# A deformable convolution sampled strip by strip: one PSUM bank for the two projection outputs, three for transposes, and a new order around the third sampling run

## What is computed

```
fine = groupnorm(x); coarse_up = bilinear_resize(coarse, 64x64)
attn = sigmoid(mean(fine) @ attend_w)
fine_cal = (fine * (attn + 1)) @ select_w
align = concat(fine_cal, 2*coarse_up) @ offset_w
om = conv3x3(align, om_w) + om_b           # 8 groups x 9 taps x (dy, dx, mask)
val[k] = sigmoid(mask_k) * bilinear(coarse_up, pixel + tap_k + offset_k)
aligned = sum_k val[k] @ dcn_w[k] + dcn_b
out = x + relu(aligned) + fine_cal
```

## Time and profile before

| what | us |
|---|---|
| median of 3 runs (3738.88 to 12106.46) | 3746.47 |
| the profiled execution | 3750.21 |
| its span | 3748.5 |
| TensorE matmul busy | 3383.5 (90%) |
| VectorE busy | 2643.4 (71%) |
| ScalarE busy | 1636.7 (44%) |
| GpSimd busy | 1300.2 (35%) |

### The profile page before, as it was taken

How to read it: one execution, slowest core, us unless ns; L and a number is a source line. 1 busy time by engine, 2 the same in 40 slices (tenths; PEclk the granted TensorE clock), 3 DMA queues, 4 the chain that set the end, 5 groups by cost and what they waited for, 6 DMA issues and landing times.

```text
span 3748.5 us, 103646 instructions
## 1 busy us (share of the span) xinstructions
PE 3383.5 (90%) x39276; PEld 3082.7 (82%) x39276; DVE 2643.4 (71%) x4029; ACT 1636.7 (44%) x3018; POOL 1300.2 (35%) x1358
## 2 busy tenths in 40 slices
PE   8979999999999947998888998998899898988998
PEld 7869999999999936888787887887788787877888
DVE  3446666666666548878876887886887887688882
ACT  0021211211221215656654665664666665566663
POOL 1000000000000025645645555554654655455451
PEclk9989999999999978999998999998999998999998
DMA  4232232222223221111112111112111112111110
GB/s 160 78 122 42 48 72 42 48 53 39 51 51 43 32 49 30 29 32 31 31 32 32 32 33 29 31 34 32 29 33 31 30 34 36 25 33 32 31 27 23
DMA packets 352248, 159.43 MB, mean 43 GB/s; under 512 B 228724, under 2 KB 346884, under 8 KB 351620
## 3 DMA queue, kind: packets, MB, share of 16 engines
q1 hardware_dynamic: 325456, 109.56, 17.4%
q10 hardware_dynamic: 21724, 26.37, 2.1%
q0 software_dynamic: 4608, 16.78, 1.2%
HBM read 104.60 MB, written 55.23 MB: 43 GB/s over the span
## 4 chain that ended last, share of the span: by engine, by line
PE 44%; issue 7%; ACT 6%; DVE 2%; POOL 2%; ACTq 1%; DMA 1%; SPq 1%; POOLq 0%; DVEq 0%
PE eb L1420 25%; PE tb L981 9%; PE vb L1003 9%; ACT wtT L986 4%; ACT ot L1025 1%; ACT res L1012 1%; DVE wt L975 1%; PE tb L911 1%; DMA win<-cpad 1%; ACTq L1316 1%; PE vb L1018 1%; ACT val L1289 1%; ACTq L882 0%; DVE val L1362 0%; SPq L1083 0%
## 5 line engine op out<-in xcount | busy, mean ns | idle before, releaser
L1420 PE MATMUL eb<-val,wd 128*128 128x256 f32 (+2 forms) x8172 | 1269.5, 300 | 9.5 <-POOL gate L1212 8.5
L1420 PEld LDWEIGHTS eb<-val,wd 128*128 128x128 f32 x8172 | 1080.6, 199 | 44.8 <-issue 35.4
L975 DVE TENSOR_TENSOR wt<-taps_all 128x576 f32<-128x576 f32 x1024 | 938.6, 984 | 52.5 <-PE tb L981 44.6
L981 PE MATMUL tb<-ident,wt 128*128 128x128 f32 x4608 | 715.9, 282 | 63.8 <-ACT wtT L986 45.3
L986 ACT COPY wtT<-tb 128x512 f32<-128x512 f32 x1152 | 651.8, 593 | 164.8 <-PE tb L981 126.0
L1362 DVE TENSOR_TENSOR val<-vb,val 128x432 fp32r<-128x432 f32 (+1 forms) x768 | 382.6, 552 | 411.0 <-ACT val L1289 409.2
L981 PEld LDWEIGHTS tb<-ident,wt 128*128 128x128 f32 x4608 | 504.7, 141 | 185.5 <-ACT wtT L986 103.6
L1289 ACT CAST val<-vb 128x432 fp32r<-128x432 f32 (+1 forms) x768 | 342.1, 524 | 706.4 <-PE vb L1003 706.2
L480 PE MATMUL conv<-fine,wf 128*108 128x256 f32 x4608 | 591.1, 289 | 7.6 <-DVE omT L751 7.6
L480 PEld LDWEIGHTS conv<-fine,wf 128*108 128x108 f32 x4608 | 570.5, 173 | 23.0 <-issue 23.0
L1003 PE MATMUL vb<-wtT,win 64*32 64x144 f32 x16384 | 350.2, 309 | 184.3 <-issue 93.3
(11 more groups left out here) (138 smaller groups left out, 3175.7 us busy)
## 6 DMA issues: line engine op xcount, KB each, us to landing
win<-cpad SPq DMA_DIRECT2D x304, 64.0 KB
om_s<-om_d SPq DMA_DIRECT2D x1152, 12.0 KB
chunk<-in_x SPq DMA_DIRECT2D x32, 512.0 KB, 5.9
xchunk<-in_x SPq DMA_DIRECT2D x32, 512.0 KB, 4.2
r_d<-r POOLq DMA_DIRECT2D x32, 512.0 KB, 3.2
rt<-r_d SPq DMA_DIRECT2D x63, 256.0 KB, 2.9
out<-ot ACTq DMA_DIRECT2D x63, 256.0 KB, 2.2
om_d<-omT SPq DMA_DIRECT2D x64, 216.0 KB
```

The costliest lines, as they stand in the source:

```text
L975: return nc.vector.tensor_tensor(wt[:, g * NK:(g + 1) * NK, WQ * u:WQ * (u + 1)].rearrange("p k (a b) -> p k a b", a=WIN), of_group(0).uns ...
L981: last = nc.tensor.transpose(tb[b][:, 128 * j:128 * j + 128], wt[:, 4 * i + j, :], ident[:])
L1420: done = nc.tensor.matmul(eb[fo][:, W * r0:W * r1], wd[wp][:, half, k, 128 * fo:128 * fo + 128], source[:, at:at + r1 - r0, cols], start=f ...
```

## The change

- `eb`: the two projection outputs share one bank, 256 columns each. Only the first matmul of output 0 has the start flag and only the last of output 1 the stop flag. `tb` gets the third bank; batch i uses bank i % 3 and waits for the copy of batch i - 3.
- `val` has ten rows; a strip's rows are 2 to 5 or 6 to 9, and rows 0 and 1 repeat rows 8 and 9. The four rows that a tap row reads are then always adjacent: no projection is split in two. The repeat is made by four DMAs on SP's queue every second strip (`duplicate_rows`), which wait for `sides` and `old_read`; `open_strip` of the even strips waits for `duplicated`. "Below" copies and `held` go, crossing copies are four in place of six.
- PE's half-slot: runs 0 and 1; transpose batches 0, 1, 2; 18 projections; wait for `val_lo`; run 2; batches 3 to 8 with no projection between them.
- `place` and `weigh` leave GpSimd. The same nine operations are issued on VectorE (`locate`) at the end of u = 1, with `hi` laid over `om`.
- Tables for the vertical positions hold 16 strips in place of 64. The general path (used when offsets are large, not run here) is adapted to the new layout.

```diff
-        VROWS, VCOLS = 9, W + 2
+        VROWS, VCOLS = 10, W + 2
...
-        tb = [bank(f"tb{i}") for i in range(2)]
+        tb = [bank(f"tb{i}") for i in range(3)]
...
-        eb = [bank(f"eb{i}") for i in range(2)]
+        eb_all = bank("eb")
+        eb = [eb_all[:, 256 * fo:256 * fo + 256] for fo in range(CH)]
...
-            LATE, KEPT = 8, 8
+            DUPLICATES = 2 * CH
+            LATE, KEPT, FIRST = 18, 18, 3
...
+                def duplicate_rows(s):
+
+                    done, read = (4 * s, s - 1) if isinstance(s, int) else (sp.to_reg(4 * s), sp.to_reg(s - 1))
+                    sp.wait_ge(consts, CONSTS)
+                    w(sp, "sides", done)
+                    w(sp, "old_read", read)
+                    for v in val:
+                        for half in range(CH):
+                            sp.dma_start(v[:, half, 0:6, 0:2].bitcast(f32), v[:, half, 0:6, 8:10].bitcast(f32)).then_inc(sems["duplicated"], 16)
...
                     elif known(s - 1, 0, ST):
+                        if turn is None or turn % 2 == 0:
+                            duplicate_rows(s)
                         w(sp, "summed", s - 1)
...
-                    if p == 1 and known(s, 0, ST):
+                    above, under = slice(0, 3), slice(6, 9)
+                    if p == 0 and (not isinstance(s, int) or 2 <= s <= ST):
+                        h(pool, "duplicated", 8 * DUPLICATES * s)
+                    if crossing is not None:
                         for v in val:
-                            g.tensor_copy(v[:, :, 3:6, 0], v[:, :, 3:6, 8].bitcast(f32)).then_inc(sems["below"], 1)
-                        h(pool, "below", s + 1)
...
                         side(s, p, 0)
-                        place(s + 2)
-                        weigh(s + 2, p)
                         measure(s + 2, p, 0)
...
+                def locate(s, p):
+                    if known(s, 0, ST):
+                        h(dve, "dist_ready", 4 * s)
+                        h(dve, "masked", s + 1)
+                        positions(dve, nc.vector, s, sems["pchain"], NPOS * s)
+                        h(dve, "pchain", NPOS * (s + 1))
+                        nc.vector.tensor_tensor(coef[p][:], lo[:, 0], mask[:], ALU.mult).then_inc(sems["coef_ready"], 1)
...
                     else:
                         for g in range(3):
                             product(s + 1, 1 - p, 0, g)
+                        locate(s + 2, p)
...
-                        pieces = ((0, 2, 7), (2, 4, 1)) if dy == 0 and q == 0 else ((0, 4, dy - 1 if q == 0 else 3 + dy),)
...
-                        for piece, (r0, r1, at) in enumerate(pieces):
-                            done = nc.tensor.matmul(eb[fo][:, W * r0:W * r1], wd[wp][:, half, k, 128 * fo:128 * fo + 128],
-                                                    source[:, at:at + r1 - r0, cols], start=first and piece == 0, stop=last)
+                        at = dy + 4 * q
+                        done = nc.tensor.matmul(eb[fo][:, 0:rows], wd[wp][:, half, k, 128 * fo:128 * fo + 128],
+                                                source[:, at:at + rows // W, cols], start=first and fo == 0, stop=last)
...
                     if u:
-                        if known(s - 1, 0, ST + 1):
-                            project(s - 1, 1 - p, todo[OLD:OLD + LATE])
-                    elif known(s - 2, 0, ST + 1):
-                        project(s - 2, p, todo[len(todo) - 2 * KEPT:len(todo) - KEPT])
-                    if sampling:
-                        h(pe, "val_lo", 6 * (n - 1) + 2)
-                        sample_blocks(2, window).then_inc(sems["sampled"], 1)
-                    if u:
-                        rest = todo[OLD + LATE:len(todo) - 2 * KEPT]
-                        target, q = s - 1, 1 - p
+                        rest, target, q = todo[OLD:len(todo) - KEPT], s - 1, 1 - p
                     else:
-                        rest = todo[len(todo) - KEPT:]
-                        target, q = s - 2, p
-                    steps = NT if u else 4
+                        rest, target, q = todo[len(todo) - KEPT:], s - 2, p
+                    owed = known(target, 0, ST + 1)
                     for i in range(NT):
+                        if i == FIRST:
+                            if owed:
+                                last = project(target, q, rest[0:LATE])
+                                if u == 0 and LATE >= len(rest):
+                                    last.then_inc(sems["projected"], 1)
+                            if sampling:
+                                h(pe, "val_lo", 6 * (n - 1) + 2)
+                                sample_blocks(2, window).then_inc(sems["sampled"], 1)
                         if known(s, 0, ST):
                             w(pe, "products", 8 * n + 2 * ((4 * i + 3) // NK + 1))
-                            w(pe, "tb_out", batch_no(s, u, i) - 1)
-                            transpose_batch(i, bank_no(s, p, u, i)).then_inc(sems["batched"], 1)
+                            w(pe, "tb_out", batch_no(s, u, i) - (0 if u and i == 0 else 2))
+                            transpose_batch(i, bank_no(i)).then_inc(sems["batched"], 1)
```

More of the change, by code:

```diff
@@ L830, in sample_and_project @@
         val = [v[:].rearrange("p (h k y x) -> p h k y x", h=CH, k=NK, y=VROWS) for v in val_all]
-        held = [sb(f"held{q}", [128, CH, 3, VCOLS], f32r) for q in range(2)]
         res = sb("res", [128, CH, 256])
@@ L1032, in fast @@
             names = ("om_loaded masked pchain coef_ready dist_ready achain capped products batched tb_out based "
-                     "win_first win_ready sampled val_hi val_lo cleared sides below entered crossed ready old_read projected finished "
-                     "r_ready summed turned ob_out out_stored").split()
+                     "win_first win_ready sampled val_hi val_lo cleared sides entered crossed ready old_read projected finished "
+                     "r_ready summed turned ob_out out_stored duplicated").split()
             sems = {n: sem("f_" + n) for n in names}
@@ L1174, in side @@
                         h(pool, "val_lo", 6 * (2 * s + hx + 1))
[L1175 removed]
+                        rows = slice(2 + 4 * p, 6 + 4 * p)
                         west, east = slice(0, NK, 3), slice(2, NK, 3)
@@ L1385, in dve_fast @@
                 bx = base_x[:].rearrange("p s (u v) -> p s v u", u=3)
-                for table, n, end, done in ((by, ST, H - 1, 8), (bx, 2, W - 1, 12)):
+                for table, n, end, done in ((by, SI, H - 1, 8), (bx, 2, W - 1, 12)):
                     own = table[:, :, 1, 0]
                     wide = lambda t: t.unsqueeze(2).broadcast_to([128, n, 3])
-                    at_end, at_start = edge[:, 0:n, 0], edge[:, 0:n, 1]
+                    at_end, at_start = (tap[1][:, 0, 0:n, end] for end in range(2))
                     dve.wait_ge(based, done)
@@ L1395, in dve_fast @@
                     nc.vector.tensor_tensor(table[:, :, 2], table[:, :, 1], wide(at_start), ALU.subtract).then_inc(based, 1)
+                dve.wait_ge(based, BASED)
+                for s in range(2):
+                    locate(s, s)
                 cap(0, 0, 0)
@@ L1495, in general @@
             parts = [val_all[q][:, 0:CH * NSUM].rearrange("p (h m) -> p h m", h=CH) for q in range(2)]
-            sums = [taps_all[:, 2:4].rearrange("p q t g a -> p (q t g a)"), win_all[:, 128:128 + NSUM]]
+            spare = [tap[q].rearrange("p t g a -> p (t g a)") for q in range(1, 4)] + [win_all[:, 128:128 + NSUM // 2]]
+            sums = [[spare[2 * half + hx].rearrange("p (k y x) -> p k y x", k=NK, y=4) for hx in range(2)] for half in range(CH)]
             def w(e, name, v):
@@ L1551, in dve_general @@
                     w(dve, "coef_ready", s + 1)
-                    for half in range(CH):
-                        nc.vector.memset(sums[half], 0.0).then_inc(sems["zeroed"], 1)
+                    for tile in spare:
+                        nc.vector.memset(tile, 0.0).then_inc(sems["zeroed"], 1)
                     with dve.Fori(0, NWIN) as wy:
@@ L1618, in pe_general @@
                         last = nc.tensor.matmul(eb[fo][:, 0:256], wd[wp][:, half, k, 128 * fo:128 * fo + 128],
-                                                parts[vp][:, half, 256 * k:256 * k + 256], start=(half == 0 and k == 0 and part == 0),
-                                                stop=(half == CH - 1 and k == NK - 1 and part == 2))
+                                                parts[vp][:, half, 256 * k:256 * k + 256], start=(half == 0 and k == 0 and part == 0 and fo == 0),
+                                                stop=(half == CH - 1 and k == NK - 1 and part == 2 and fo == CH - 1))
                     last.then_inc(sems["projected"], 1)
```

115 lines of the change are left out of this document (48 added, 67 removed).

## The result

| | us | ratio to before, 95% interval |
|---|---|---|
| before, on the same chip | 3743.3 | |
| changed, median (3806.21 to 3817.0) | 3810.89 | 1.0185 [1.0162, 1.0208] |
| changed, profiled execution (span 3804.5, clock 0.943) | 3806.21 | |

A forecast was written before the change was run, and what follows sets the result against it. TensorE was taken as the bound, with gaps, its idle time behind X. From 3750.2 us, +10 (order and projections), +28 (clock), -22 (crossings), +4 (image starts), -4 (stage start) gave 3766, stated as 3763 for the median; range 3650 to 3860.

The forecast's parts named there:

- Part 1, the split projections: Odd strips' projection runs on TensorE fall from 108 to 72 matmuls: gain 3.67 us every two strips; bank alternation entered at 0.
- Part 2, the pacing: TensorE's new order, paced by ScalarE's copies, costs 4.0 us over four half-slots; with the split projections' gain, +10 us in all.
- X: Moment in a TensorE half-slot when the third sampling run has been issued and a transpose batch starts; forecast 5.9 us after start.
- Part 3, the clock: TensorE's longer wait before odd first halves slows its clock in half the turns: +28 us, ends 0 and +74.
- the branch: TensorE's wait at the loop's turn, where the last batch starts 4.08 us ahead of the next sampling; taken to stay.
- Part 3, transposes keep the clock: Transpose batches behind X without projections between them keep TensorE's clock: nothing entered; by the skill's rule some +190 us.
- Part 4, positions: Nine position operations take about 3.3 us a strip on VectorE, against 9.95 on GpSimd; nothing entered.
- the tie: First halves: VectorE's subtractions free the first banks at X + 12.6, just when TensorE wants the third run; nothing entered.
- Part 5: Carried rows by DMA entered at 0; batch crossings give back 22 us, image starts cost 4, stage start gives back 4.
- The new order is free: Rival, chance 0.2: ScalarE's pacing falls away, 3607 us; decided by sampling starting less than X + 6 in second halves.
- VectorE becomes the bound: Rival, chance 0.24: third runs of first halves wait behind positions and two products; 3835 us if positions take 5 us.
- The clock falls in every half-slot: Rival, chance 0.08: transposes do not keep TensorE's clock, three more falls a turn at 2.4 us, about 3955 us.

The follow-up runs named there:

- run 3: The changed kernel with the nine operations of the positions back on GpSimd: 3815.41 us.
- run 11: The changed kernel with TensorE's order of before, positions on GpSimd, and transpose batches waiting as with two banks though three exist: 3649.88 us.
- Runs 12 to 15: Extra matmuls ahead of the loop: changed kernel by 20, 3824.48 us; kernel before by 20, 3760.09; changed by 100, 3774.42; changed by 72, 3720.18.
- Run 8: The changed kernel with the 18 projections right behind sampling runs 0 and 1, ahead of transpose batches 0 to 2: 3799.97 us.
- runs 2 and 9: Changed kernel with 8 projections and no batch ahead of the third run, 10 projections after batches 0 to 2, 3697.91 us; with TensorE's order of before, 3695.85 us.
- e15_two_turns_shifted: The changed kernel with TensorE's order of before, positions on GpSimd, TensorE's loop body doubled and 100 more matmuls ahead of the loop: 3527.21 us.

## Why the forecast was wrong

- **Part 1, the split projections: right.** Runs of 72 take 9.0 us in both parities; forecast 8.9. The alternation of outputs in one bank costs nothing that shows.
- **Part 2, the pacing: right to 0.4 us in each place.** Forecast were X + 5.9, + 7.3 and + 8.4. X comes 5.95 us behind the start (2407.79 to 2413.74); from X to the 72 projections 5.5 us (2431.23 to 2436.72), to sampling 7.2 (2451.59 to 2458.78), at the turn 8.15 (2413.74 to 2421.89). The sum of the new order and its third bank, run 3's kernel against run 11's (both have the positions on GpSimd and the pause): 3815 - 3650 = 165 us, forecast 124 + 28 + 4 = 156.
- **Part 3, the clock: the step that failed.** It took the slow start behind the turn from the earlier trace rows as it was, 2.4 us, "At the loop's turn TensorE waits 3.1 to 3.6 us, and the 96 sampling matmuls behind it mostly take 3.13 us", and entered new falls only for odd first halves. Those came much as forecast (18 of 28 are slow, +1.3 us a turn in place of 0.9), though the wait's length alone does not decide: two starts ahead of the loop, behind waits of 2.6 and 2.8 us, were fast. But behind the turn the excess over a half-slot without slow start grew from 1.5 to 3.9 us up to the fourth batch (11.27 against 7.40; before 5.05 against 3.59 up to X). Of this growth 1.2 us is the pause, and the rest fits the slow clock (0.61 of full speed over the first 8 us, 0.79 before). Runs 12 to 15 show that it is no matter of the clock alone nor of the order: it is where the loop's code lies. What the forecast put at nothing is the time in which TensorE fetches its code behind the jump; it had "the branch" as a wait that "stays". With the code in the other place the changed kernel takes 3720. The forecast lies between the two, 48 below the one and 43 above the other, and the sum of waits that the forecast made holds nothing by which to choose: how near it came, either way, is luck.
- **Part 3, transposes keep the clock: right.** The 72 projections of a first half start right behind 24 transposes and the four of the offsets, with no projection among them, and all 63 such runs of the changed kernel took the fast time, 8.97 to 9.13 us. Run 8 moved the transposes away from the slow sampling for 11 us. The rule of the Trainium skill ("TensorE: Matmul & The Clock Gate", Part 4) would have had a fall in every half-slot; none of these 63 first halves shows one ahead of its projections.
- **Part 4, positions: right for this order, and for the reason given.** They take 3.0 us in VectorE's timeline (forecast 3.3), and the tie held:

```profile
2419.20 0.29 DVE L937 TENSOR_TENSOR pos<-om,base_y 128x144 f32<-128x144 f32 x1
...
2421.87 0.31 DVE L1331 TENSOR_TENSOR coef<-lo,mask 128x144 f32<-128x144 f32 x1
2422.42 3.07 DVE L975 TENSOR_TENSOR wt<-taps_all 128x576 f32<-128x576 f32 x2 [0.24 <-issue]
```

  Only in TensorE's old order, with less work ahead of the third run, do they cost 111 us.
- **Part 5: right.** The DMAs land in 5.9 us and nobody waits for them. Crossings gave back 35 us (forecast 22), image starts cost 11 (forecast 4), and the stage's start, up to 1,565 us, gave back 3 (forecast 4).
- **The rivals.** "The new order is free" fell at its own point (sampling at X + 7.2, not under X + 6). "VectorE becomes the bound" did not happen here (1.6 us of waiting in all) but did in runs 2 and 9, in 32 first halves each, by up to 2.8 us. "The clock falls in every half-slot" fell with the 63 fast runs.

## What to carry to other kernels

Work that fills a wait is worth more than its place in a list suggests: ten projections, moved from ahead of the run that ScalarE waits for to behind it, were worth 146 us. When two edits delay the same point, undo both before you call one free. And when a tight loop's time moves by one or two per cent with no wait to explain it, look behind the jump for a pause at a fixed count of instructions and shift the code once: here that was 91 us. Here the pause ended some 2.7 us after the first matmul behind the jump, wherever it began, so a place that TensorE reaches later than that cost nothing.

## What the runs showed of the hardware

- **The pause behind a jump.** It comes after a fixed number of matmuls and moves one for one with the code: from the 61st to the 41st for a shift by 20, and to the 89th for a shift by 100, that is 61 - 100 + 128 (in run `e15_two_turns_shifted` 59 - 100 + 128 = 87). Each matmul has its weight load, so 128 matmuls are 256 instructions. The page's list of DMA queues has one for instructions (queue, kind: packets, MB, share of 16 engines):

```profile
q8 instruction: 360, 5.90, 0.7%
```

  5.90 MB in 360 packets are 16.4 KB each, which fits one packet for 256 instructions of 64 bytes. The trace has the time of every packet of this queue, and they settle what TensorE waits for. In the changed kernel, in 25 of 25 turns, the first matmul behind the jump starts 1.95 to 2.17 us after the end of one packet; the packet, about 1.1 us, and these 2 us nearly fill the wait of 3.1 to 3.7 us that the timeline puts down to "issue". The next packet begins about when that matmul does, and the pause ends 1.21 to 1.47 us after that packet has ended. With the pause at the 41st, the 89th and the 95th matmul the second distance is 1.18 to 1.56 us. The Trainium skill says the same of the mechanism ("Runtime: NRT & Kernel Launch", Instruction fetch mechanics): instructions come in blocks of 16 KiB, fetched ahead in sequence, and a taken branch breaks that; it has no price; here the pause took from 0.2 to 2.3 us, start to start.
- **Its size depends on its place, its end does not**: from one matmul's start to the next it takes on average 1.8 us at the 41st, 1.2 at the 61st, 1.1 at the 89th (16 of 25 turns) and 0.8 at the 95th in the kernel before (16 of 25), and there is none where it would be the 117th. The matmul behind it starts 2.6 to 2.7 us after the first one behind the jump in all four, on average. (The 0.9 and 1.4 of the expectations are idle times and not start to start.)
- **VectorE beside GpSimd's distances.** Two products take 3.07 us where six ran in 4.16 just before, 1.5 us each against 0.7. GpSimd's timeline shows what is beside them:

```profile
2422.04 1.18 POOL L950 TENSOR_TENSOR taps_all<-pos,ctr_x 128x576 f32<-128x576 f32 x1 [5.38 <-DVE lo L945]
2423.18 1.70 POOL L950 TENSOR_TENSOR taps_all<-pos,ctr_y 128x576 f32<-128x576 f32 x1
```

  Over 1,560 to 3,600 us of this trace, 544 products with nothing on GpSimd beside them took 745 ns each, with ScalarE busy or not; 118 with GpSimd busy all along took 1,195 on average.
